# Sparse expert blocks as two halves of 256 slots: an 8-expert mixture stage on one core

## The reference, cut to what matters

```python
logits = xf @ w_router                      # 8 experts
probs = softmax(logits); topk_w, topk_idx = top_k(probs, 2)
weights = sum(topk_w[..., None] * one_hot(topk_idx, 8))
h = gelu(einsum('te,ieh->tih', xf, w1) + b1)      # 128 -> 512
out = einsum('tih,ihe->tie', h, w2) + b2          # 512 -> 128
out = sum(out * weights[..., None], axis=1)
x = x + 0.5 * out
```

## Time and profile before

| what | value |
|---|---|
| median of 3 runs | 1467.69 us (1464.27 to 1469.27) |
| span of the profiled execution | 1464.5 us |
| PE busy (matmuls) | 1277.9 us, 87% |
| DVE busy | 1149.4 us, 78% |
| ACT busy | 887.0 us, 61% |
| POOL busy | 520.0 us, 36% |
| mean granted PE clock | 0.954 |

### The profile page before, as it was taken

The page is one execution under the profiler, slowest core; times in us unless marked ns, Lnnn a source line. Parts: engine busy times, 40 slices in busy tenths (PEclk is TensorE's granted clock), DMA queues, the critical chain, the costliest instruction groups (busy, mean ns, idle before and its releaser), DMA issues.

```text
span 1464.5 us, 20418 instructions
## 1 busy us (share of the span) xinstructions
PE 1277.9 (87%) x6496; PEld 766.6 (52%) x6496; DVE 1149.4 (78%) x2430; ACT 887.0 (61%) x1402; POOL 520.0 (36%) x757
## 2 busy tenths in 40 slices
PE   6768999779999889998679999899999889899998
PEld 5557777412222222222267777666666345566665
DVE  6857879789889989889466989878886664877875
ACT  6846767348788768887577667633333477334432
POOL 6773427444534424511273335514430120210100
PEclk9989999779999989999889999999999999999999
DMA  8521453332212202210151122255453011054434
GB/s 285 143 86 52 151 196 117 129 90 86 86 45 88 86 24 91 92 35 2 66 224 56 58 73 86 78 126 114 105 118 73 13 32 24 1 127 107 92 84 116
DMA packets 88679, 133.94 MB, mean 91 GB/s; under 512 B 16756, under 2 KB 42836, under 8 KB 87548
## 3 DMA queue, kind: packets, MB, share of 16 engines
q1 hardware_dynamic: 81404, 117.93, 28.5%
q0 software_dynamic: 7168, 14.69, 3.4%
HBM read 82.23 MB, written 47.45 MB: 89 GB/s over the span
## 4 chain that ended last, share of the span: by engine, by line
PE 55%; DVE 25%; issue 8%; ACT 7%; DMA 3%; POOL 1%; SPq 1%; DVEq 0%; ACTq 0%; POOLq 0%
DVE shared L2170 6%; PE bank L1557 6%; PE pair L904 5%; PE pair L906 5%; PE pair L905 5%; PE bank L2248 5%; PE pair L1469 3%; PE pair L1471 3%; PE pair L1470 3%; PE pair L2230 3%; PE pair L2162 3%; DVE shared L960 3%; ACT shared L2238 2%; DVE shared L1545 1%; PE bank L974 1%
## 5 line engine op out<-in xcount | busy, mean ns | idle before, releaser
L2170 DVE TENSOR_REDUCE shared<-pair 128x2 f32<-128x1024 f32 x256 | 309.7, 1217 | 41.6 <-PE pair L2162 38.7
L2238 ACT ACTIVATE shared<-pair 128x1024 f32<-128x1024 f32 x256 | 260.5, 1022 | 51.7 <-PE pair L2230 50.2
L960 DVE TENSOR_TENSOR shared<-shared 128x512 fp32r<-128x512 f32 x232 | 193.2, 842 | 76.9 <-ACT shared L950 73.4
L904 PE MATMUL pair<-shared 128*128 128x512 f32 x464 | 198.2, 427 | 9.9 <-DMA shared<-w_keep 3.9
L1524 ACT ACTIVATE shared<-pair 128x512 f32<-128x512 f32 x144 | 85.6, 596 | 179.5 <-PE pair L1471 179.3
L906 PE MATMUL pair<-shared 128*128 128x512 f32 x464 | 187.3, 404 | 0.0
L905 PE MATMUL pair<-shared 128*128 128x512 f32 x464 | 187.3, 404 | 0.0
L945 ACT ACTIVATE shared<-pair,shared 128x512 f32<-128x512 f32 x168 | 115.9, 690 | 72.7 <-PE pair L906 67.3
L1469 PE MATMUL pair<-shared 128*128 128x512 f32 x288 | 154.4, 536 | 4.9 <-DVE shared L1479 4.9
L2248 PE MATMUL bank<-shared 128*9 128x512 f32 x1024 | 139.6, 618 | 4.5 <-ACT shared L2238 4.3
L277 POOL DMA_INDIRECT staged<-ys_rows,slots x112 | 117.7, 1051 | 58.4 <-ACT shared L2238 32.1
(11 more groups left out here) (380 smaller groups left out, 2262.7 us busy)
## 6 DMA issues: line engine op xcount, KB each, us to landing
shared<-p_coef_rows SPq DMA_DIRECT2D x64, 512.0 KB, 6.0
shared<-xs_rows SPq DMA_DIRECT2D x42, 256.0 KB, 2.8
ys_rows<-shared SPq DMA_DIRECT2D x42, 256.0 KB, 2.0
w_keep<-shared SPq DMA_DIRECT2D x8, 1024.0 KB, 4.8
shared<-w_keep SPq DMA_DIRECT2D x16, 512.0 KB, 9.6
shared<-p_q_parts SPq DMA_DIRECT2D x64, 96.0 KB, 2.4
shared<-p_k_parts SPq DMA_DIRECT2D x64, 96.0 KB, 2.5
xs_rows<-shared SPq DMA_DIRECT2D x1, 5376.0 KB, 18.4
```

The costliest lines, as they stand in the source:

```text
L904: nc.tensor.matmul(out_bank, w_hi, x_hi, start=start, stop=False)
L960: nc.vector.tensor_tensor(hl[u % RING][:], hid[u % RING][:], hh[u % RING][:], ALU.subtract).then_inc(s["dve_done"], 1)
L2170: nc.vector.tensor_reduce(mneg[:, i, 2 * c:2 * c + 2], pair_of("max", b, m)[:], AX_X, ALU.max, negate=True).then_inc(s["mx_read"], 1)
L2238: nc.scalar.activation(probs[st % 2][:, 2 * p:2 * p + 2, :], pair_of("exp", b, 2 * st + p)[:], ACT.Exp, scale=scale).then_inc(s["exp_done" ...
```

## The change

A block of 512 slots is now two halves of 256, and each half has an expert of its own (`NSUB` = 36 halves, `NBLK` = 18 blocks and not 21, since less padding is needed). Of a sparse unit's work, what depends on the expert is done by half: `up0` and `down0` issue two triples of matmuls of 256 columns where there was one of 512, with weights of their own; `gelu0` and `y_act` run twice on 256 columns with another bias column. Chunk `c` of a sparse unit is now half `c // 2`, hidden features `2 * (c % 2)` and the one behind it. POOL copies the weights per half, so twice for a block, and a buffer changes hands each half. Splitting (`xh`, `xl`, `hh`, `hl`), both transposes and the copies of results stay at 512 columns. Loads and stores move the same bytes of a block, with the rows dealt out by half. The tables of experts and biases have 36 columns.

```diff
-NBLK = (2 * (B - 1) * T + NE0 * (T - 1)) // T
+HB = T // 2
+NSUB = (2 * (B - 1) * T + NE0 * (HB - 1)) // HB
+NBLK = (NSUB + 1) // 2
+NSUB = 2 * NBLK
...
-        past_e, ex_g, ex_all = sb("past_e", [P, NBLK, NE0]), sb("ex_g", [P, NBLK]), sb("ex_all", [P, NBLK])
+        past_e, ex_g, ex_all = sb("past_e", [P, NSUB, NE0]), sb("ex_g", [P, NSUB]), sb("ex_all", [P, NSUB])
...
+            def taken(what, h):
+                order = [("up", 0)]
+                for k in range(NSUB + 2):
+                    order += [("up", k + 1)] if k + 1 < NSUB else []
+                    order += [("down", k - 2)] if k > 1 else []
+                return 2 * NSUB * occ + order.index((what, h)) + 1
+            def sub(i, c):
+                return 2 * (i - D) + c // 2
...
             def up0(i, c):
-                    else:
-                        nc.tensor.wait_ge(s["w_taken"], 2 * NBLK * occ + max(1, 2 * (i - D)))
+                if not dense(i) and c % 2 == 0:
+                    nc.tensor.wait_ge(s["w_taken"], taken("up", sub(i, c)))
...
+                if not dense(i):
+                    w, at = w_up[sub(i, c) % 2], slice(c // 2 * HB, (c // 2 + 1) * HB)
+                    for k in range(2):
+                        m = 2 * (c % 2) + k
+                        last = hi_lo(bank[u % 4][:, k * HB:(k + 1) * HB], w[:, m * P:(m + 1) * P], w[:, HID + m * P:HID + (m + 1) * P],
+                                     xh[q][:, at], xl[q][:, at], True, True)
+                    last.then_inc(s["up_ready"], 1)
+                    return
...
             def down0(i, c):
+                    w, at = w_down[sub(i, c) % 2], slice(c // 2 * HB, (c // 2 + 1) * HB)
+                    for k in range(2):
+                        m, of = 2 * (c % 2) + k, slice(k * HB, (k + 1) * HB)
+                        last = hi_lo(bank[4 + i % 2][:, at], w[:, m * P:(m + 1) * P], w[:, HID + m * P:HID + (m + 1) * P],
+                                     hh[u % RING][:, of], hl[u % RING][:, of], m == 0, m == HC - 1)
...
             def gelu0(i, c):
+                for k in range(2):
+                    at, col = slice(k * HB, (k + 1) * HB), (2 * (c % 2) + k) * NSUB + sub(i, c)
+                    last = nc.scalar.activation(hid[u % RING][:, at], bank[u % 4][:, at], ACT.Gelu_apprx_tanh, bias=bias_t[:, col:col + 1])
...
             def take_up(g, j, ex_):
                 if j > 1:
-                    g.wait_ge(s["up_ready"], U0 + HC * (D + j - 1))
+                    g.wait_ge(s["up_ready"], U0 + HC * D + 2 * (j - 1))
...
-            GATHERS = {14: ((1, 0),), 15: ((1, 1), (1, 2)), 16: ((1, 3),), 17: ((2, 0), (2, 1)), 18: ((2, 2),), 19: ((2, 3),)}
+            GATHERS = {NSUB - 14 + (3 * k) // 2: (1 + k // TILES, k % TILES) for k in range(2 * TILES)}
...
-                for j in range(NBLK):
-                    e1 = nc.gpsimd.value_load(expert_t[0:1, j + 1:j + 2], min_val=0, max_val=NE0 - 1) if j + 1 < NBLK else None
-                    if j + 1 < NBLK:
-                        take_up(g, j + 1, e1)
-                    take_down(g, j, ex_)
-                    ex_ = e1
+                for j in range(NSUB + 2):
+                    if j + 1 < NSUB:
+                        of[j + 1] = nc.gpsimd.value_load(expert_t[0:1, j + 1:j + 2], min_val=0, max_val=NE0 - 1)
+                        take_up(g, j + 1, of[j + 1])
+                    if j > 1:
+                        take_down(g, j - 2, of.pop(j - 2))
...
                 def rows(v, i):
-                    return v[i * T:(i + 1) * T, :].rearrange("(p k) e -> p (k e)", k=TILES)
+                    return v[i * T:(i + 1) * T, :].rearrange("(h p k) e -> p h (k e)", h=2, k=TILES // 2)
...
             def early_act(i, c):
-                    nc.scalar.wait_ge(moe0_sems["w_taken"], 2 * NBLK * (occ0 + 1))
+                    nc.scalar.wait_ge(moe0_sems["w_taken"], 2 * NSUB * (occ0 + 1))
```

More of the change, by code:

```diff
@@ L729, in biases @@
                 for c in range(HC + 1):
-                    last = nc.tensor.matmul(bank[6][:, c * NBLK:(c + 1) * NBLK], b_rows[:, c * P:(c + 1) * P], onehot[:], start=True, stop=True)
+                    last = nc.tensor.matmul(bank[6][:, c * NSUB:(c + 1) * NSUB], b_rows[:, c * P:(c + 1) * P], onehot[:], start=True, stop=True)
                 last.then_inc(s["pe_step"], 1)
@@ L926, in down0 @@
                 nc.tensor.wait_ge(s["dve_done"], dve_no("hl", i, c))
-                if c == 0:
-                    if not dense(i):
-                        nc.tensor.wait_ge(s["w_taken"], 2 * NBLK * occ + min(2 * (i - D) + 3, 2 * NBLK))
-                    if i > 1:
-                        nc.tensor.wait_ge(s["act_done"], act_no("y", i - 2))
-                w = w_all[:, i * 4 * HID + 2 * HID:(i + 1) * 4 * HID] if dense(i) else w_down[(i - D) % 2]
+                if c == 0 and i > 1:
+                    nc.tensor.wait_ge(s["act_done"], act_no("y", i - 2))
+                if not dense(i):
+                    if c % 2 == 0:
+                        nc.tensor.wait_ge(s["w_taken"], taken("down", sub(i, c)))
+                    w, at = w_down[sub(i, c) % 2], slice(c // 2 * HB, (c // 2 + 1) * HB)
[3 more added lines that the diff above has]
+                                     hh[u % RING][:, of], hl[u % RING][:, of], m == 0, m == HC - 1)
+                    last.then_inc(s["down_done"], 1)
+                    return
+                w = w_all[:, i * 4 * HID + 2 * HID:(i + 1) * 4 * HID]
                 hi_lo(bank[4 + i % 2][:], w[:, c * P:(c + 1) * P], w[:, HID + c * P:HID + (c + 1) * P], hh[u % RING][:], hl[u % RING][:], c == 0,
@@ L965, in y_act @@
                     nc.scalar.wait_ge(s["yback"], ALL * occ + i - 1)
-                bias = vecs[:, V_B2 + i:V_B2 + i + 1] if dense(i) else bias_t[:, HC * NBLK + i - D:HC * NBLK + i - D + 1]
-                nc.scalar.activation(yT[i % 2][:], bank[4 + i % 2][:], ACT.Identity, bias=bias).then_inc(s["act_done"], 1)
+                if dense(i):
+                    nc.scalar.activation(yT[i % 2][:], bank[4 + i % 2][:], ACT.Identity, bias=vecs[:, V_B2 + i:V_B2 + i + 1]).then_inc(s["act_done"], 1)
+                    return
+                for k in range(2):
+                    at, col = slice(k * HB, (k + 1) * HB), HC * NSUB + 2 * (i - D) + k
+                    last = nc.scalar.activation(yT[i % 2][:, at], bank[4 + i % 2][:, at], ACT.Identity, bias=bias_t[:, col:col + 1])
+                last.then_inc(s["act_done"], 1)
             def back_pe(i):
@@ L1293, in gpsimd @@
                         last.then_inc(tables_ready, 1)
-                    if D + j == NORM - 2:
+                    if j == 2 * (NORM - 2 - D):
                         norm_b(f)
-                    for b, tile in GATHERS.get(j, ()):
+                    if j in GATHERS:
+                        b, tile = GATHERS[j]
                         stored_by(g, occ, b)
@@ L1334, in x_load @@
                         q_.wait_ge(s["xT_ps"], PREPS * occ + i - 1)
-                    q_.dma_start(xb[i % 3], rows(xs_rows, i)).then_inc(s[f"x_ld{i % 3}"], 16)
+                    q_.dma_start(halves(xb[i % 3]), rows(xs_rows, i)).then_inc(s[f"x_ld{i % 3}"], 16)
                 x_load(0)
@@ L1348, in sync @@
                     q_.wait_ge(s["dve_done"], dve_no("y", D + i))
-                    q_.dma_start(rows(ys_rows, i), yb[i % 2]).then_inc(y_stored[i % 2], 16)
+                    q_.dma_start(rows(ys_rows, i), halves(yb[i % 2])).then_inc(y_stored[i % 2], 16)
                     if occ == 0 and 2 < i < 3 + NE0:
```

57 lines of the change are left out of this document (30 added, 27 removed).

## The result

The changed kernel takes 1495.93 us (median of four executions, 1490.29 to 1498.1) beside 1468.48 for the kernel before (1464.27 to 1472.2): a ratio of 1.019, 95% interval 1.016 to 1.022, so slower by some 2%. Measured once more in a later comparison (experiment 9) it took 1491.4 beside 1468.1, ratio 1.016 (1.012 to 1.019). The forecast was 1464.7 us, with a range up to 1490.

The account below looks back on a forecast made before the run. The prediction took PE to pace steady blocks before and DVE after: 24.1 us for slower blocks - 38.6 for removed blocks + 4 + 2.5 + 4.0 + 1 = -3.0, so 1464.7 us, range 1445 to 1490.

Parts of the forecast that it names:

- the first of the four extra costs: Extra work in DVE's queue, such as `combine`, stops PE in full: 0 to 3.6 us per stage, 4 us taken.
- the forecast's own pace of 7.1 us: Steady sparse blocks: DVE sets 7.1 us per block after the change, where a block took 6.43 before.
- all four costs: Beside the block pace: DVE queue work 4 us, gathers 2.5, end-of-stage wait 4.0, `past_e` 1.
- Removed blocks: Both sparse stages: three blocks fewer in each, 6 x 6.43 = 38.6 us saved.
- PE per block: Sparse blocks: 48 narrow matmuls at 0.124 us plus transposes make 6.83 us, 6.42 from below; loads overlap products.
- DVE per block: Sparse blocks: four POOL copies cost DVE 0.62 us each, upper bound 1.05; 7.1 us, DVE sets the pace.
- Two of the signs: Expected in the profile's steady blocks: mean of `hl_dve` near 1.3 us and not 0.997; DVE over 95% busy.
- Gathers: Gather rounds on POOL: copies and DMAs take 11.3 us against 10.65; 0 to 2.6 per stage, 2.5 together.
- End wait: End of first stage: ACT's wait for all weight copies delays the last gelus; 4.0 us, bounds 0 and 6.
- `past_e`: Expert table: comparison of 36 and not 21 columns, at most 3.4 us; 1 us taken.
- The second: Rival: DVE loses more to copies in `hl_dve`, blocks from 7.31 us; 1483 us at 0.75 a copy; chance 0.30.
- Weights come late: Rival: DVE stretches POOL's copies to 1.3 us in gather rounds, costing 17 us, 1479 us; chance 0.06.

Follow-up runs that it names:

- experiment 9: Changed kernel as it is, measured once more: 1491.4 us beside 1468.1 for the kernel before, ratio 1.016.
- experiment 6: Kernel before, with products, gelus and bias steps of sparse blocks done in two halves of 256 columns: 1473.6 us, ratio 1.005.
- experiment 3: Kernel before, with every weight copy made twice, one after the other: 1516.97 us, ratio 1.034.
- experiment 11: Kernel before, with the third chunk's conversion of each sparse block made by ACT and not DVE: 1466.79 us, ratio 0.998.
- experiment 5: Kernel before, with every weight copy behind the first two of each kind cut from 1024 to 64 columns: 1448.84 us, ratio 0.989.
- experiment 7: Changed kernel, with the third chunk's conversion of each sparse block made by ACT and not DVE: 1477.89 us, ratio 1.010 to the kernel before.
- experiment 10: Changed kernel, with each weight copy of 1024 columns made as four of 256: 1490.48 us, ratio 1.015 to the kernel before.
- Experiment 12: Changed kernel, with each down copy waiting for one more unit of products, apart from the up copy: 1476.57 us, ratio 1.006 to the kernel before.

## Why the prediction was wrong

The step that failed is the first of the four extra costs, "with no slack left, work put into DVE's queue stops PE in full. Most of it does already": taken at 4 us in all. Over PE's pace stalls grew by 39.1 us, and over the forecast's own pace of 7.1 us still by 22.6 (33 blocks at 7.1 and not 6.6 take up 16.5 of it); with 15.9 us of longer tails that is 38.5, where all four costs were put at 11.5. Most of it did not stop PE already: the stalls of the kernel before got longer, and new ones came behind the gathers. In it are 5.6 us of PE's wait for a late weight copy in stage 2 and 4.0 of the one for ACT; nearly all other waits that grew are for DVE. The mechanism was named, copies on POOL against DVE, but its effect was put into the pace of the steady blocks at one mean price, as if the slower engine were never kept waiting. In stage 1 of the changed kernel PE is idle 19.6 us of 136.4, and DVE 21.1.

- **Removed blocks**, 38.6 us: taken over into the sum above, six blocks at 6.43; no run measures it by itself.
- **PE per block**, 0.124 us per narrow product and 6.83 us: 0.118 and 6.6. The lower half of the bounds; experiment 6 confirms that narrow work costs only some 0.2 us a block. The load is hidden. The rule of the Trainium skill, "TensorE: Matmul & The Clock Gate", section "Part 3: Packing small matmuls — row/col tiling", that loads overlap only where row groups differ, is so contradicted by the narrow products too: all use all rows and start 0.118 us apart. The same section also names a load into the background weight buffer as one that is pulled ahead of matmuls in flight; no run here shows whether that is at work.
- **DVE per block**, 0.62 us a copy, 7.1 us, "DVE, not PE, sets the pace": the price was somewhat high as a mean. Over a whole stage a copy costs 0.51 to 0.55 in three kernels (0.55 after, 0.52 before, and (132.13 - 94.75) / 73 = 0.51 in experiment 3), which makes 6.9 us a block, still over PE's 6.6. Wrong was to make a steady pace of it: PE does single blocks in 6.6 us and then waits for DVE in blocks of 11 to 12.6 us. And the price is not one number: steps from PSUM lose nothing, in a train a copy costs 1.02, its upper bound in the forecast. Two of the signs show the same: low parts take 1.004 us on average and not 1.3, and over the blocks of stage 1 DVE is busy 85% and not over 95%.
- **What a full DVE means.** Here lies the error. A block that PE does in 6.6 us looks free. But a stage has half a dozen places with more DVE work (the weights' table, the norm, the projections' weights, the gathers' combining), and each leaves DVE late. In the kernel before it is back within a block or two (experiment 11: more free time doesn't help), and 16 us is all that the copies cost (experiment 5). In the changed kernel the same places cost more, and the norm's own steps take 2.6 us and not 1.1. Experiments 3 and 7, doubling the copies and taking one step off DVE, show from both sides that DVE's load sets the stalls. That DVE isn't back in time between two places is argued and not the whole of it: with 1.2 us free a block, experiment 7 still has twice the stalls of the kernel before.
- **Gathers**, 2.5 us, as too little of POOL's time, with weights that come late: POOL was short of time there, and from 221.76 to 239.65 it works all but without a pause; DVE pays for it, by the trains. Not foreseen were the 4.60 and 7.69 us that POOL stood at the first gather; in stage 2 they made weights come 5.6 us late for PE, once. Moving the gathers gave 8.8 us in the profiled stages.
- **End wait**, 4.0 us: PE waited exactly 4.0 us there, but moving the wait gave 1 to 3 us, as DVE was late next.
- **`past_e`**, 1 us: not seen; the first transposes of stage 1 start at 110.03 us and not 109.95, and the attention stretch ahead of stage 2's routing is 1.5 us shorter.
- **The rivals.** The second, a greater loss of DVE, had the sign and the range's upper part, and the trains are its mechanism; but it made a steady block of over 7.31 us of it, where there are single blocks of 6.6 and stalls. "Weights come late" is 5.6 us of stage 2, by POOL's wait at the first gather and not by slower copies, and it is what experiment 10 made of the whole kernel.

Left open: how much of the 22 us is trains and how much plain number. Experiment 12 was to tell that and didn't, since the trains stayed; the 13.6 us of stalls behind the gathers, without extra work, are as far as the block times go. What sets the clock of the last stretch (0.98 before, 0.94 and 0.97 in the two profiles of the changed kernel, 0.95 in experiment 11) isn't settled either.

## What to carry to other kernels

When an engine comes out at 99% in a steady block, don't price it at nothing because the block still fits: count its steps there, list the places where it gets extra work, and ask how late it is behind each. Two sums over the whole stage point to it: by the forecast's own numbers DVE has 21 x 5.83 = 122 us of block work per stage before and 18 x 7.1 = 128 after, more work in less time. In stage 1, as measured, the copies take 14 us of DVE more (33.9 and not 19.7), and the three blocks give back 13 (94.75 to 81.38 without copies). A cost that one engine puts on another counts as the other's work, and its price is to be read where the two meet most: trains of copies cost twice the mean.

## What was not expected of the hardware

A DVE step met by POOL copies can stand for a whole train: a conversion of 0.42 us took 2.53 beside two copies, 4.43 beside four, about 1.0 us a copy, where the mean over a stage is half of that. Cut into quarters the same copies cost DVE 0.23 us and not 0.55, and POOL 2.0 us and not 1.05 to 1.2: the loss moves to the other engine. On average a POOL copy of 64 columns took 0.35 us and one of 256 some 0.5, where 1024 take 1.05 at the least: a copy doesn't get shorter in proportion. A stall of PE was followed by a granted clock of 0.79 in the block behind it, which made that block 8.20 us long where 6.6 is usual. Not every stall was: in the kernel before, the block behind the one of 9.75 us (from 143.30) ran at 1.00 and took 6.43.
